# Attention's products with V in two bursts of four key tiles instead of three bursts

## Chip, cores and metric

The kernel runs on one core of one Trainium2 chip. The metric is the device time of one launch in microseconds, median of several runs; less is better.

## What is computed

The input is x, (8, 1024, 512) in float32, with a conditioning vector of 1024 for each of the 8 batch items. Two layers follow each other. The first is attention with 16 heads of 32 channels; the second is a selective state-space (Mamba) layer with 1024 inner channels and 16 states. The change touches the first alone:

```python
xn = layer_norm(x, norm_w, norm_b)
q = (xn @ q_w + q_b).reshape(Bx, Tx, H, -1)
k = (xn @ k_w + k_b).reshape(Bx, Tx, H, -1)
att = jnp.einsum('bnhl,bmhl->bnmh', q, k)
att = att + (1.0 - mask) * -1000000.0
att = jax.nn.softmax(att, axis=2)
v = ((xn @ v_w + v_b) * src_mask[:, :, None]).reshape(Bx, Tx, H, -1)
y = jnp.einsum('bnmh,bmhl->bnhl', att, v).reshape(Bx, Tx, Dx)
```

After it come a layer norm with scale and shift by the conditioning, silu, the product with out_w, the residual, and the second layer (in-projection, convolution over 4 rows, the scan over 1024 rows for 16 states, gate, out-projection).

## The kernel before, in words

Everything is float32. The 8 batch items ("instances") are worked one after the other by a loop on every engine. One instance has these stages in order: attention, norm and out-projection, norm and in-projection, convolution, dt projection, then two scan halves (dg 0 and 1) of 16 states each. Under the scan of one instance run, spread over its steps, the gate and out-projection of the instance before (dg 0) and the norm and Q, K, V products of the next one (dg 1). The queues wait for each other by semaphores written out by hand; no scheduler moves anything.

Attention is a software pipeline of 128 steps (16 heads times 8 tiles of 128 queries), which runs in step with itself on three engines. In step s:

- TensorE (line 1338 on) takes the scores of tile s: two matmuls 128x512 into one of two pairs of PSUM banks (L1316 to 1326, after the wait L1322 for the maximum of tile s-2, whose bank pair it reuses). Then it transposes the probabilities of tile s-3, eight blocks 128x128 in two quads of four (L1347), one quad for VectorE to copy out and one for ScalarE. Then come products with V (L1358 to 1361). Then, in one step of four, one transposition of the finished output (L1369).
- VectorE (L1046 on) adds the mask to the scores of tile s-1 and takes their minimum in one instruction (L1053), then, in one step of four, the normalisation of a finished output (L1063) or, in another, its copy out of PSUM (L1073) and a reciprocal (L1076), and last it copies its quad of transposed probabilities of tile s-3 (L1083).
- ScalarE (L817 on) takes the exponential of tile s-1 (L821) and copies its quad of tile s-3 (L830).

The quads go through a ring of three PSUM banks (RING, L38 on), in the order VectorE's quad of a tile, ScalarE's quad of it, and after each fourth tile one bank for the transposed output. A quad can be written when the copy of the use three places earlier is done (ring_free, L1328). So in the step after that extra use, ScalarE's quad has to wait for ScalarE's own copy of the tile before.

Four query tiles make a half (512 queries) of one head. Its product with V is y^T = V^T P^T: for each of 8 key tiles m and 4 query tiles c one matmul of V's 32 columns against a 128x128 block of P^T, into a quarter of the partitions of PSUM bank 6: 32 instructions a half. (The profile shows two records for each of them, so x24 is 12 instructions.) `AV_KEYS` (L58) says which key tiles are taken in the four steps after a half's last probabilities are copied. The four steps are named by their place in that tuple: step 0 (s mod 4 = 3) has three key tiles, step 1 three, step 2 two, step 3 none, and in step 3 the output is transposed. When key tile 7 is done, `s_av` is signalled; VectorE waits for it at L1070 before its copy L1073.

```python
                        for m in AV_KEYS[step]:
                            for c in range(HG):
                                last = mm(ps[c * HD:(c + 1) * HD, 6, 0:P], V[:, m, head * HD:(head + 1) * HD],
                                          PT[:, half % 2, m, c * P:(c + 1) * P], m, NT - 1)
                        if NT - 1 in AV_KEYS[step]:
                            last.then_inc(s_av.sem, 1)
```

L1238 is the line of the helper `mm`; the scores and the products with V both carry it and are told apart by their tiles: ps<-k_stack,q_stack is a score, ps<-area_h,area_u a product with V.

Of the kernel before, what the change touches and what calls it, by code (L numbers as in the profile page):

```python
# [54 lines left out]
def ring_bank(*use):  # L55

    return RING[RING_AT[use] % len(RING)]
AV_KEYS = ((0, 1, 2), (3, 4, 5), (6, 7), ())  # L58


N0_STEP, QKV_STEP = 13, 17
# [103 lines left out]
def build(nc, x, condT, mask, params, q_w, k_w, v_w, v_b, emb_w, emb_b, out_w, out_b,  # L165
          adaT, ada_b, inT, xpT, dtT, D_row, opT, out):
    ctx = ExitStack()
    with ctx:
# [1065 lines left out]
        def _(pe):  # L1234
# [80 lines left out]
            with pe.Fori(0, B) as b:  # L1315
# [22 lines left out]
                for s in range(ALL + Y_LAG):  # L1338
# [13 lines left out]
                    if HALF - 1 <= t < ALL + HALF - 1:  # L1352
                        half, step = (t - HALF + 1) // HALF, (t - HALF + 1) % HALF
                        head = half // 2
                        if step == 0:
                            pe.wait_ge(*s_pv.at(b, (half + 1) * HALF))
                            pe.wait_ge(*s_pa.at(b, (half + 1) * HALF))
# [6 lines that stand above are left out]
# [195 lines left out]
```

## Time and profile before

| | |
|---|---|
| median of 3 runs | 7165.17 us (7164.62 to 7170.4) |
| the profiled execution, its own time | 7160.22 us |
| its span | 7158.7 us |
| busy, share of the span | PE 88%, PEld 56%, DVE 83%, ACT 66%, POOL 44% |
| mean granted TensorE clock | 0.934 |
| products with V (x16384 records) | 603.2 us busy |
| transposes of the probabilities (x8192) | 1131.7 us busy |
| scores (x2048) | 746.7 us busy |
| masked minimum on VectorE (x1024) | 1242.5 us busy |
| exponential on ScalarE (x1024) | 1177.6 us busy |

The span is the stretch from the first to the last instruction of one execution; busy times are sums over it. PE is TensorE's matmuls (their ends are modelled), PEld its weight loads, which overlap them; DVE is VectorE, ACT ScalarE. Attention takes a stretch of some 270 us in each instance, the first from about 211 us to 487 us.

### The profile page before, as it was taken

How to read it: one execution, taken by the hardware profiler on the slowest of the kernel's cores; microseconds unless marked ns; L12 is line 12 of the kernel's file. 1: busy time of each engine (PE TensorE's matmuls, PEld its weight loads, DVE VectorE, ACT ScalarE, POOL GpSimd, SP SyncE). 2: the span in 40 equal slices, each digit the busy share in tenths (PEclk: the TensorE clock that was granted, in tenths of full speed). 3: DMA queues.
4: the chain of work that ended last, by engine and by line, in shares of the span. 5: the costliest groups of instructions: out<-in, count | busy, mean ns of one | idle time of the engine just before them, and what ended most of it. 6: DMA issues, size and time to landing. Idle time of an engine off the chain costs nothing.

```text
span 7158.7 us, 136172 instructions
## 1 busy us (share of the span) xinstructions
PE 6334.7 (88%) x43360; PEld 4004.7 (56%) x43360; DVE 5937.4 (83%) x7137; ACT 4693.5 (66%) x6673; POOL 3146.6 (44%) x1533
## 2 busy tenths in 40 slices
PE   6998799987999879989799888998799987999878
PEld 2664457644575546745467445764457544575544
DVE  0778989799896998969988799878989799896995
ACT  2665678666685667846777467766678566685664
POOL 0105771067601874018730388105771077601873
PEclk9999899998999989999799998999899998999979
DMA  3425783367923777238762487425783367823776
GB/s 142 150 91 160 178 201 118 115 160 167 238 67 135 166 173 204 72 137 189 179 169 87 137 202 186 136 96 154 178 203 115 120 158 168 233 66 136 168 174 174
DMA packets 432957, 1092.13 MB, mean 153 GB/s; under 512 B 50056, under 2 KB 50184, under 8 KB 428000
## 3 DMA queue, kind: packets, MB, share of 16 engines
q1 hardware_dynamic: 256672, 671.49, 28.5%
q0 software_dynamic: 157120, 378.04, 27.3%
q10 hardware_dynamic: 18432, 33.56, 1.3%
q8 instruction: 371, 6.08, 0.3%
q14 instruction: 362, 2.97, 0.1%
HBM read 564.39 MB, written 250.10 MB: 114 GB/s over the span
## 4 chain that ended last, share of the span: by engine, by line
PE 64%; issue 14%; DVE 8%; POOL 5%; ACT 5%; DMA 3%; SPq 1%; DVEq 1%; ACTq 0%; POOLq 0%
PE ps L1238 39%; PE ps L1483 11%; PE ps L1347 7%; POOL area_s L695 4%; PE ps L1288 3%; ACT area_h L830 2%; DVE area_h L1161 2%; DMA z_keep<-z_st 2%; DVE area_s L1053 2%; PE ps L1290 1%; ACT area_s L821 1%; DVE area_dt L1149 1%; PE ps L1432 1%; DMA area_acc<-area_w 1%; ACT k_stack L798 1%
## 5 line engine op out<-in xcount | busy, mean ns | idle before, releaser
L695 POOL TENSOR_TENSOR area_s<-area_u,area_s 128x1024 f32<-128x1024 f32 x1024 | 2536.6, 2546 | 666.3 <-DVE area_u L1152 387.0
L1161 DVE TENSOR_TENSOR_SCAN area_h<-ps,area_s 128x1024 f32<-128x1024 f32 x1024 | 2333.3, 2279 | 28.4 <-POOL area_s L695 15.0
L1483 PEld LDWEIGHTS ps<-ident,area_h 128*128 128x128 f32 x8192 | 1008.7, 151 | 961.0 <-DVE area_acc L1171 484.9
L1483 PE MATMUL ps<-ident,area_h 128*128 128x128 f32 x8192 | 1201.6, 294 | 382.1 <-DVE area_h L1161 205.7
L821 ACT ACTIVATE area_s<-area_s,negmax 128x1024 f32<-128x1024 f32 x1024 | 1177.6, 1150 | 406.6 <-DVE negmax L1053 406.1
L1053 DVE CUSTOM_DVE_ANT_0 area_s<-ps,area_dt 128x1024 f32<-128x1024 f32 x1024 | 1242.5, 1214 | 106.7 <-PE ps L1238 104.8
L888 ACT ACTIVATE ps<-area_dt,negA 128x1024 f32<-128x1024 f32 x1024 | 1145.9, 1120 | 240.3 <-DVE area_h L1161 120.9
L682 POOL TENSOR_TENSOR area_s<-area_s 128x1024 f32<-128x1024 f32 x64 | 176.1, 2752 | 2495.9 <-ACT area_s L861 2495.9
L874 ACT ACTIVATE area_w<-ps,C_nat 128x512 f32<-128x512 f32 x1024 | 703.8, 687 | 824.7 <-PE ps L1483 811.6
L1347 PE MATMUL ps<-ident,area_s 128*128 128x128 f32 x8192 | 1131.7, 277 | 35.9 <-ACT area_s L821 18.7
L1347 PEld LDWEIGHTS ps<-ident,area_s 128*128 128x128 f32 x8192 | 941.0, 142 | 267.6 <-ACT area_h L830 74.1
L1238 PE MATMUL ps<-area_xT,area_w 128*128 128x512 f32 x2176 | 1011.4, 600 | 57.9 <-ACT k_stack L798 39.4
L1171 DVE SCALAR_TENSOR_TENSOR area_acc<-ps,C_nat,area_acc 128x512 f32<-128x512 f32 x1024 | 746.4, 729 | 202.1 <-PE ps L1483 201.8
L1083 DVE COPY area_h<-ps 128x512 f32<-128x512 f32 x1024 | 705.2, 689 | 244.7 <-PE ps L1347 244.6
L1238 PE MATMUL ps<-k_stack,q_stack 128*128 128x512 f32 x2048 | 746.7, 446 | 15.3 <-DVE negmax L1053 12.1
L1238 PE MATMUL ps<-area_w,area_xT 128*128 128x512 f32 x1536 | 713.6, 600 | 0.4 <-ACT area_xT L766 0.4
L1238 PEld LDWEIGHTS ps<-area_xT,area_w 128*128 128x128 f32 x2176 | 395.3, 191 | 501.3 <-issue 356.8
L1238 PE MATMUL ps<-area_h,area_u 128*32 128x128 f32 x16384 | 603.2, 277 | 7.3 <-ACT area_h L830 7.3
L830 ACT ACTIVATE area_h<-ps 128x512 f32<-128x512 f32 x1024 | 590.4, 577 | 11.7 <-PE ps L1347 11.6
L1118 DVE SCALAR_TENSOR_TENSOR area_h<-area_h,par 128x1024 f32<-128x1024 f32 x192 | 372.6, 1940 | 167.1 <-ACT area_h L852 162.5
L1238 PEld LDWEIGHTS ps<-area_h,area_u 128*32 128x32 f32 x16384 | 401.9, 109 | 134.1 <-issue 127.0
L712 POOL DMA_DIRECT2D area_acc<-area_w x256 | 341.6, 1334 | 267.9 <-ACT area_w L874 159.7
(125 smaller groups left out, 5560.2 us busy)
## 6 DMA issues: line engine op xcount, KB each, us to landing
area_acc<-area_w POOLq DMA_DIRECT2D x256, 1024.0 KB, 8.7
area_s<-b_rows SPq DMA_DIRECT2D x256, 512.0 KB, 5.0
q_stack<-qk_keep SPq DMA_DIRECT2D x520, 128.0 KB, 2.7
k_stack<-qk_keep SPq DMA_DIRECT2D x520, 128.0 KB, 3.2
qk_keep<-q_stack SPq DMA_DIRECT2D x144, 256.0 KB, 5.0
qk_keep<-k_stack SPq DMA_DIRECT2D x144, 256.0 KB, 5.3
area_s<-z_keep SPq DMA_DIRECT2D x72, 512.0 KB, 4.5
y_keep<-area_acc POOLq DMA_DIRECT2D x8, 4096.0 KB, 14.6
```

The source lines that it names most:

```text
L695: pool.tensor_tensor(dbu[:, dl % 2, :], U[:, k // (NS * DL) * DL + dl, :], bb[:, q, :], ALU.mult).then_inc(s_dbu.sem, 1)
L821: nc.scalar.activation(S[:, t % SR, :], S[:, t % SR, :], ACT.Exp, scale=-1.0, bias=negmax[:, t % TILES:t % TILES + 1], accum_out=den[:, t ...
L830: nc.scalar.activation(PT[:, (t // HALF) % 2, HALF:NT, c * P:(c + 1) * P], ps[:, ring_bank("act", t), :].rearrange("p (m c) -> p m c", m=H ...
L874: nc.scalar.activation(part[slot][:, n // 2, :], ps[:, 5, :], ACT.Identity, scale=C_nat[:, n, columns(r, 1)]).then_inc(s_ev.sem, 1)
L888: nc.scalar.activation(banks(2 * (dl % 2)), dT[:, dl, :], ACT.Exp, scale=negA[:, a_col:a_col + 1]).then_inc(s_da.sem, 1)
L1053: v.tensor_tensor_reduce(out=S[:, t % SR, :], in0=banks(2 * (t % 2)), in1=mask_add, scale=-1.0, scalar=3.0e38, op0=ALU.add, op1=ALU.min, a ...
L1083: v.tensor_copy(PT[:, (t // HALF) % 2, 0:HALF, c * P:(c + 1) * P], ps[:, ring_bank("dve", t), :].rearrange("p (m c) -> p m c", m=HALF)).th ...
L1161: v.tensor_tensor_scan(out=hs[:, q, dl, :], data0=banks(2 * (dl % 2)), data1=dbu[:, dl % 2, :], initial=0.0, op0=ALU.mult, op1=ALU.add).th ...
L1171: v.scalar_tensor_tensor(out=part, in0=ps[:, 4, :], scalar=c_col, in1=part, op0=ALU.mult, op1=ALU.add).then_inc(s_acc.sem, 1)
L1238: return nc.tensor.matmul(out, lhsT, rhs, start=(k == 0), stop=(k == last))
L1347: last = nc.tensor.transpose(ps[:, ring_bank(who, t), m * P:(m + 1) * P], S[:, t % SR, (c * HALF + m) * P:(c * HALF + m + 1) * P], ident[: ...
L1483: last = nc.tensor.transpose(ps[:, 4 + n % 2, dl * P:(dl + 1) * P], hs[:, r % 2, dl, n * P:(n + 1) * P], ident[:, :])
```

## The change

One line, the table of key tiles by step:

```diff
@@ -55,7 +55,7 @@
-AV_KEYS = ((0, 1, 2), (3, 4, 5), (6, 7), ())
+AV_KEYS = ((0, 1, 2, 3), (), (4, 5, 6, 7), ())
```

The order of VectorE, ScalarE, GpSimd and the DMA queues is the same before and after. TensorE's order in attention, steps 1 to 3 of a half, was this before (the register instruction at L1322 is the wait ahead of the scores, the one at L1367 that ahead of the output's transposition; ps<-k_stack,q_stack are scores, ps<-ident,area_s transposes of probabilities, ps<-area_h,area_u products with V, ps<-ident,area_w the output's transposition):

```order
L1238 MATMUL ps<-k_stack,q_stack 128x512 x2
L1347 MATMUL ps<-ident,area_s 128x128 x8
L1238 MATMUL ps<-area_h,area_u 32x128 x12
L1322 REGISTER_ALU
L1238 MATMUL ps<-k_stack,q_stack 128x512 x2
L1347 MATMUL ps<-ident,area_s 128x128 x8
L1238 MATMUL ps<-area_h,area_u 32x128 x8
L1322 REGISTER_ALU
L1238 MATMUL ps<-k_stack,q_stack 128x512 x2
L1347 MATMUL ps<-ident,area_s 128x128 x8
L1367 REGISTER_ALU
L1369 MATMUL ps<-ident,area_w 128x128
```

The burst of step 0 is just ahead of the first of these rows, at x12. Of the changed kernel the same three steps read so, with a burst of x16 just ahead of the first row:

```order
L1238 MATMUL ps<-k_stack,q_stack 128x512 x2
L1347 MATMUL ps<-ident,area_s 128x128 x8
L1322 REGISTER_ALU
L1238 MATMUL ps<-k_stack,q_stack 128x512 x2
L1347 MATMUL ps<-ident,area_s 128x128 x8
L1238 MATMUL ps<-area_h,area_u 32x128 x16
L1322 REGISTER_ALU
L1238 MATMUL ps<-k_stack,q_stack 128x512 x2
L1347 MATMUL ps<-ident,area_s 128x128 x8
L1367 REGISTER_ALU
L1369 MATMUL ps<-ident,area_w 128x128
```

Step 1 has lost its burst of twelve; steps 0 and 2 hold sixteen each. The count of instructions is the same, and every matmul accumulates in the same order as before.

## Rows read from the trace of the kernel before

**Rows 1.** Busy time by stretch: span, PE, PEld, DVE, ACT, POOL busy; PEclk; DMA share, GB/s
```profile
215.00:477.00 262.00, 259.25 (x3184) 198.41 (x3183) 236.59 (x461) 212.72 (x372) 21.48 (x15) 1.00 0.30 90
...
600.00:700.00 100.00, 77.21 (x350) 46.15 (x349) 87.75 (x63) 60.59 (x71) 61.58 (x29) 0.88 0.49 130
...
1200.00:1300.00 100.00, 99.20 (x1234) 75.86 (x1225) 89.92 (x176) 80.52 (x142) 0.00 (x0) 1.00 0.23 64
```

**Rows 2.** Waits, 215 to 477 us: engine and line, releaser, us in total, times, longest
```profile
DVE area_h L1083 <- PE ps L1347: 25.3, 60, 0.5
...
PEld ps L1347 <- ACT area_h L830: 8.9, 29, 0.4
```

**Rows 3.** Timeline of PE: start, us, engine, line, op, tiles, count [idle before <-releaser]
```profile
1202.49 0.73 PE L1238 MATMUL ps<-k_stack,q_stack 128*128 128x512 f32 x2
1203.06 1.04 PE L1347 MATMUL ps<-ident,area_s 128*128 128x128 f32 x8
...
1204.02 0.64 PE L1238 MATMUL ps<-area_h,area_u 128*32 128x128 f32 x16
1204.60 0.73 PE L1238 MATMUL ps<-k_stack,q_stack 128*128 128x512 f32 x2
1205.17 1.04 PE L1347 MATMUL ps<-ident,area_s 128*128 128x128 f32 x8
...
1206.04 0.27 PE L1369 MATMUL ps<-ident,area_w 128*128 128x128 f32 x1
1206.07 0.71 PE L1238 MATMUL ps<-k_stack,q_stack 128*128 128x512 f32 x2
...
1206.64 1.35 PE L1347 MATMUL ps<-ident,area_s 128*128 128x128 f32 x8
...
1207.33 0.42 PEld L1347 LDWEIGHTS ps<-ident,area_s 128*128 128x128 f32 x4 [0.30 <-ACT area_h L830]
...
1207.92 0.86 PE L1238 MATMUL ps<-area_h,area_u 128*32 128x128 f32 x24
1208.72 0.73 PE L1238 MATMUL ps<-k_stack,q_stack 128*128 128x512 f32 x2
...
1210.25 0.86 PE L1238 MATMUL ps<-area_h,area_u 128*32 128x128 f32 x24
...
1211.04 0.73 PE L1238 MATMUL ps<-k_stack,q_stack 128*128 128x512 f32 x2
```

**Rows 4.** The same timeline, VectorE and ScalarE
```profile
1203.69 0.69 DVE L1083 COPY area_h<-ps 128x512 f32<-128x512 f32 x1 [0.49 <-PE ps L1347]
...
1204.30 1.21 DVE L1053 CUSTOM_DVE_ANT_0 area_s<-ps,area_dt 128x1024 f32<-128x1024 f32 x1
...
1205.56 1.15 ACT L821 ACTIVATE area_s<-area_s,negmax 128x1024 f32<-128x1024 f32 x1 [0.60 <-DVE negmax L1053]
...
1206.71 0.58 ACT L830 ACTIVATE area_h<-ps 128x512 f32<-128x512 f32 x1
...
1209.92 0.69 DVE L1083 COPY area_h<-ps 128x512 f32<-128x512 f32 x1 [0.34 <-PE ps L1347]
```

**Rows 5.** Timeline at the start of attention, before the first product with V
```profile
214.50 1.03 PE L1347 MATMUL ps<-ident,area_s 128*128 128x128 f32 x8
...
215.29 0.71 PE L1238 MATMUL ps<-k_stack,q_stack 128*128 128x512 f32 x2
...
217.48 1.22 DVE L1053 CUSTOM_DVE_ANT_0 area_s<-ps,area_dt 128x1024 f32<-128x1024 f32 x1
...
218.62 0.68 DVE L1083 COPY area_h<-ps 128x512 f32<-128x512 f32 x1
```

**Rows 6.** Timeline, PE: scores of steps 7 and 127, then the last burst
```profile
220.50 0.73 PE L1238 MATMUL ps<-k_stack,q_stack 128*128 128x512 f32 x2
...
477.04 0.71 PE L1238 MATMUL ps<-k_stack,q_stack 128*128 128x512 f32 x2
...
484.98 1.96 PE L1238 MATMUL ps<-area_h,area_u 128*32 128x128 f32 x64 [0.67 <-ACT area_h L830]
```

## Prediction

> **What bounds the kernel now.** I read the busy time by stretch first. In attention TensorE is busy 259.25 of 262 us at a granted clock of 1.00, the upper of its two levels (2.4 GHz), VectorE 236.59 and ScalarE 212.72 [rows 1]. TensorE seems to be the bound, but VectorE has only 10% left. Then the waits of the same stretch [rows 2]: VectorE waits for transposes 60 times (25.3 us), and TensorE's weight loads wait 29 times (8.9 us) for ScalarE's copy L830. That is two VectorE waits and one TensorE wait in a half. Attention is therefore no plain queue of TensorE work but a loop through three engines, and what counts is its longest path.
>
> The timeline gives that path. I call the starts of the scores in four steps on end X0, X1, X2 and X3, where s mod 4 is 0, 1, 2 and 3. In [rows 3] X1 is 1202.49, X2 1204.60, X3 1206.07, the next X0 1208.72 and the next X1 1211.04. The rows with x24 and x16 show which step is which: for one, the burst of 24 records at 1207.92 stands ahead of 1208.72. A step runs from one start of scores to the next: the step from X1 ends with the burst of 16, the step from X2 with the output's transposition and no burst, the steps from X3 and X0 with 24 each. (In the code's tuple the steps from X1, X2, X3 and X0 are places 2, 3, 0 and 1.) The step lengths are 2.11, 1.47, 2.65 and 2.32 us, 8.55 us for a half. The step from X3 has a bank wait inside it: its transposes take 1.35 us instead of 1.04 [rows 3], so 0.31 us.
>
> The loop that makes 8.55 us, from ScalarE's copy at 1206.71 [rows 4], which frees the bank for which TensorE waits:
> - copy 1206.71 to X0 1208.72 (rest of the transposes, burst of 24): 2.01
> - X0 to X1: 2.32
> - X1 to VectorE's copy, 1202.49 to 1203.69: 1.20
> - that copy to the next masked minimum, 1203.69 to 1204.30: 0.61
> - minimum to exponential, 1204.30 to 1205.56: 1.26
> - exponential to ScalarE's next copy, 1205.56 to 1206.71: 1.15
>
> The sum is 8.55, the measured half. In the first attention the scores of step 7 start at 220.50 and those of step 127 at 477.04 [rows 6]: 256.54 us for 30 halves, 8.55 each.
>
> **The change part by part.** No instruction is added or removed; 24 records leave the step from X0, which has none left; 8 of them go to the step from X3 (24 to 32) and 16 to the step from X1 (16 to 32).
>
> *Price of a burst of 32 records*, which attention does not show. From burst to next scores, 24 records take 0.80 (1207.92 to 1208.72) and 16 take 0.58 (1204.02 to 1204.60) [rows 3]: 0.22 for 8. So 32 take 1.02. Lower end: 0.80, the burst of 24. Upper end: two bursts of 16 with their switches, 2 x 0.58 plus the 0.17 of the next item, 1.33. I take 1.02, because the last burst of 64 records is 1.96 us long [rows 6] and the one of 24 is 0.86: 1.10 for 40, or 0.22 for 8, the same slope.
>
> *Price of a step without burst and without output's transposition*: scores to transposes 0.57 (1202.49 to 1203.06), transposes to scores 0.79 at the start of attention (214.50 to 215.29) [rows 5]; 1.36 in all. Upper end: the 1.47 of the step with the output's transposition. From transposes to a burst it is 0.96 (1203.06 to 1204.02) instead of 0.79: entering a burst costs 0.17, and of the 0.58 for 16 records 0.14 is not explained by the slope (0.58 - 2 x 0.22). So each burst has about 0.31 us that its length does not set. The Trainium skill (TensorEngine Tiling (Array Packing), Key Properties) says that changing the tiling mode, not just the tile, drains TensorE. By that rule alone the change removes one visit to the 32-column mode in each half; with the 0.31 us of the rows and the old bank wait kept, a half would fall to 8.24, close to what the sum below gives by another path. No row shows the drain itself, only the 0.31 us.
>
> *TensorE's own floor afterwards*: step from X3 2.65 - 0.31 + 0.22 = 2.56, from X1 2.11 + 0.44 = 2.55, from X2 1.47, from X0 1.36: 7.94 us without any wait. Before, it was 2.34 + 2.32 + 2.11 + 1.47 = 8.24.
>
> *The old loop afterwards*: 2.01 + 0.22, then 1.36 for X0 to X1, then 1.20 + 0.61 + 1.26 + 1.15: 7.81. It no longer decides.
>
> *The loop that takes its place* goes through VectorE's queue. The step from X0 is now so short that VectorE can't finish its turn in it: its turn is 0.61 for the copy and 1.14 for the minimum (217.48 to 218.62) [rows 5], 1.75 back to back. Path: ScalarE's copy to X0, 2.23; X0 to VectorE's copy, 1208.72 to 1209.92 [rows 4], 1.20; copy to minimum 0.61; minimum to the next copy 1.14, now without waiting for transposes; copy to minimum 0.61; minimum to exponential 1.26; exponential to ScalarE's copy 1.15. The sum is **8.20 us**. (In the kernel before the same path is 7.98, below 8.55.) It is above the floor of 7.94, so a bank wait of about 0.26 us stays at the same place.
>
> So a half goes from 8.55 to 8.20, 0.35 less. 30 halves in each of 8 instances are 240: -84 us. The first seven steps hold no product with V and the tail of five steps after the last scores has one switch less, at most 0.31 us an instance, some -2 us. What else could be touched: VectorE's wait L1070 for `s_av`. The last burst in the step from X1 now ends 0.44 later against X1 (2.55 instead of 2.11), while VectorE gets to L1073 at X1 + 1.20 + 0.61 + 1.14 = 2.95 or, late by the new loop, 3.34. The margin is 0.4 us or more, so it costs nothing; if it were gone, VectorE's copy and then TensorE's next transposes would be late. The stack loads on SP's queue are released by scores and have a whole head (eight steps, over 16 us) to land; nothing is moved past them. After attention every stage starts with TensorE's or VectorE's last attention work, so it starts earlier by the same amount and I see no transfer that would hold it.
>
> Sum: 7160.22 - 86 = 7074 us for the profiled execution. The median is 4.95 us above that execution: 7165.17 - 86 = **7079 us**, 1.2% faster. About 0.2% (14 us) is what a measurement of this kernel can tell from no change.
>
> **The rivals.**
> 1. *TensorE's floor alone.* If VectorE's lateness of 0.39 us (X0 to the second minimum 1.20 + 0.61 + 1.14 + 0.61 = 3.56, against 1.36 + 1.20 + 0.61 = 3.17) is absorbed somewhere, a half is 7.94: 0.61 x 240 = -146 us, with the tail -148, so 7017 us. For it: VectorE's busy share leaves room. Against it: every link of the new loop is a start-to-start distance that the trace shows, and the same kind of sum gave 8.55 exactly.
> 2. *A burst of 32 costs like two of 16.* At 1.33 the steps from X3 and X1 are 2.34 + 0.53 = 2.87 and 2.11 + 0.75 = 2.86, the floor is 8.56, and nothing is won: 7168 us (+0.01 x 240 = +2). The burst of 64 in [rows 6] speaks against it.
> 3. *Slower: the granted clock falls.* TensorE would work in two lumps with a thin step between. The clock is 1.00 in attention with PE busy 99% [rows 1], and in a stretch where PE is busy 77% it is 0.88. If all TensorE work of attention ran at 0.88, the floor would be 7.94 / 0.88 = 9.02, +0.47 x 240 = +113 us, 7278 us. It turns slower below 7.94 / 8.55 = 0.93. Against it: TensorE's bank wait is 0.26 in 8.20 after and 0.31 in 8.55 before, the same share.
>
> **How the numbers follow.** The VectorE loop has 0.80, the floor alone 0.12, the price of two bursts 0.04, the clock 0.04. The predicted time is that of the loop, 7079. Its own range: the burst's price enters the loop once and the slopes leave 0.99 to 1.05, and each of seven links is read to 0.01, together 0.07 a half or 17 us: 7062 to 7096. The unknown's own ends reach from 7026 (at 0.80 the loop is 7.98) to 7168; I take in half of the lower side and a little of the upper: 7040 to 7100. That leaves out some 2 in 10. Faster by over 0.2%: loop and floor, 0.92. Within 0.2%: 0.04. Slower: 0.04.
>
> **What the profile afterwards would show.** Bursts of x32 with 1.02 us to the next scores; a half of 8.20 us; step lengths from X1 on about 2.55, 1.47, 2.82 (with the bank wait) and 1.36. VectorE waits for transposes once in a half instead of twice, and in the step from X1 its copy follows the minimum at once. The wait of TensorE's weight loads for L830 stays at 29 or so times an attention, 0.3 us each. If the half is 7.9 and that wait is gone, rival 1 is right; if x32 takes 1.3, rival 2; if PEclk in attention is below 0.93, rival 3. The forecast is wrong if time appears outside attention, as an idle stretch at its end that eats the gain.

## The result and the profile after

The changed kernel takes 7082.68 us in the median of 4 runs (7079.03 to 7087.21); the kernel before, measured beside it, 7164.9 us (7163.94 to 7170.4). The ratio is 0.9884, with a 95% interval of 0.9867 to 0.9901: faster by 1.2%. The forecast was 7079. The profiled execution has a span of 7083.9 us (own time 7085.44) against 7158.7, 74.8 us less, where the sum had said 86.

Busy time by stretch, changed kernel, the part of the first attention that answers to the 262 us of [rows 1] (span; PE, PEld, DVE, ACT, POOL busy; PEclk; DMA share, GB/s):

```profile
215.00:467.00 252.00, 250.14 (x3190) 200.04 (x3188) 235.13 (x460) 213.86 (x374) 21.50 (x15) 1.00 0.32 93
```

and the waits of the same stretch (engine and line, releaser, us in total, times, longest), which answers to [rows 2]:

```profile
DVE area_h L1083 <- PE ps L1347: 16.2, 30, 0.6
PEld ps L1347 <- ACT area_h L830: 8.1, 29, 0.3
```

The clock stayed at 1.00. VectorE waits for transposes 30 times instead of 60, once in a half; TensorE still waits 29 times for ScalarE's copy, 0.28 us each (8.1 us in 29) instead of 0.31 (8.9 in 29). The work of VectorE is nearly the same (235.13 us) in 252 us instead of 262: 93% busy instead of 90%.

TensorE's timeline in one half, in the manner of [rows 3] (start, us, engine, line, op, tiles, count):

```profile
1196.69 0.71 PE L1238 MATMUL ps<-k_stack,q_stack 128*128 128x512 f32 x2
...
1199.21 0.73 PE L1238 MATMUL ps<-k_stack,q_stack 128*128 128x512 f32 x2
...
1200.69 0.71 PE L1238 MATMUL ps<-k_stack,q_stack 128*128 128x512 f32 x2
...
1201.26 1.32 PE L1347 MATMUL ps<-ident,area_s 128*128 128x128 f32 x8
...
1201.92 0.42 PEld L1347 LDWEIGHTS ps<-ident,area_s 128*128 128x128 f32 x4 [0.27 <-ACT area_h L830]
...
1202.51 1.08 PE L1238 MATMUL ps<-area_h,area_u 128*32 128x128 f32 x32
...
1203.52 0.73 PE L1238 MATMUL ps<-k_stack,q_stack 128*128 128x512 f32 x2
...
1204.87 0.71 PE L1238 MATMUL ps<-k_stack,q_stack 128*128 128x512 f32 x2
```

X1 is 1196.69, X2 1199.21, X3 1200.69, X0 1203.52, X1 1204.87. The step lengths are 2.52, 1.48, 2.83 and 1.35, together 8.18 us; the forecast was 2.55, 1.47, 2.82 and 1.36. A burst of 32 records takes 1.01 us to the next scores (1202.51 to 1203.52), where I had 1.02. VectorE and ScalarE in the same half, in the manner of [rows 4]:

```profile
1196.54 0.69 DVE L1083 COPY area_h<-ps 128x512 f32<-128x512 f32 x1 [0.54 <-PE ps L1347]
...
1197.14 1.21 DVE L1053 CUSTOM_DVE_ANT_0 area_s<-ps,area_dt 128x1024 f32<-128x1024 f32 x1
...
1198.28 0.69 DVE L1083 COPY area_h<-ps 128x512 f32<-128x512 f32 x1
...
1198.89 1.21 DVE L1053 CUSTOM_DVE_ANT_0 area_s<-ps,area_dt 128x1024 f32<-128x1024 f32 x1
...
1200.14 1.16 ACT L821 ACTIVATE area_s<-area_s,negmax 128x1024 f32<-128x1024 f32 x1
...
1201.29 0.58 ACT L830 ACTIVATE area_h<-ps 128x512 f32<-128x512 f32 x1
...
1204.72 0.69 DVE L1083 COPY area_h<-ps 128x512 f32<-128x512 f32 x1 [0.53 <-PE ps L1347]
```

In the step from X1 VectorE goes from minimum (1197.14) to copy (1198.28) in 1.14 us with no wait between; its only waits are those of 0.54 and 0.53 us in the step from X0. The forecast loop, read off these rows: ScalarE's copy 1201.29 to X0 1203.52 2.23, X0 to VectorE's copy 1204.72 1.20, copy to minimum 0.60, minimum to copy 1.14, copy to minimum 0.61, minimum to exponential 1.25, exponential to ScalarE's copy 1.15. That is 8.18. It is not one lucky half: the median over 232 neighbouring pairs of scores X1, all instances together, is 8.19 us, and 8.55 in the kernel before.

Over the whole first attention the scores of steps 7 and 127 stand at

```profile
220.43 0.73 PE L1238 MATMUL ps<-k_stack,q_stack 128*128 128x512 f32 x2
```

```profile
466.07 0.72 PE L1238 MATMUL ps<-k_stack,q_stack 128*128 128x512 f32 x2
...
477.07 0.33 PE L1369 MATMUL ps<-ident,area_w 128*128 128x128 f32 x1 [1.30 <-DVE area_w L1073]
```

so 30 halves take 245.64 us, 8.19 each, 10.90 less than in [rows 6]. (The row at 477.07 is the last transposition of an output, used below.)

**Stage by stage.** Read from the starts of each stage's first and last instructions in both traces and added over the 8 instances: from the first to the last masked minimum of attention 2175.3 us before and 2090.6 after, 84.7 less; from there to the last transposition of an output 71.3 and 69.7, 1.6 less. So attention gave 86.3 us, where the sum had 86. The stage after it, up to the last transposition of norm 2, grew from 363.1 to 381.5 us, 18.4 more, and the next, in-projection and convolution, fell from 568.6 to 561.2. The rest agrees within 2 us. In this pair of executions about 11 us of the gain was given back right behind attention. From the last output transposition to the in-projection it looks like this in the kernel before:

```profile
488.23 0.33 PE L1369 MATMUL ps<-ident,area_w 128*128 128x128 f32 x1 [1.30 <-DVE area_w L1073]
490.96 3.28 PE L1260 MATMUL ps<-ident,area_dt 128*128 128x128 f32 x16 [2.40 <-DVE area_dt L1024]
...
535.74 35.46 PE L1238 MATMUL ps<-area_xT,area_w 128*128 128x512 f32 x82 [1.64 <-ACT area_xT L766]
```

That is 47.51 us (488.23 to 535.74), and in the changed kernel (477.07 above to the row below) 49.30:

```profile
526.37 34.17 PE L1238 MATMUL ps<-area_xT,area_w 128*128 128x512 f32 x79 [1.08 <-ACT area_xT L766]
```

No instruction of this stage was changed. The granted clock did change. Here are two stretches of 10 us that hold most of the transposes of norm 1 and the second half of those of norm 2, kernel before (PEclk is the third number from the end):

```profile
491.00:501.00 10.00, 7.82 (x35) 6.72 (x36) 5.00 (x15) 6.83 (x10) 0.00 (x0) 0.69 0.56 211
531.00:541.00 10.00, 7.22 (x29) 4.12 (x30) 1.09 (x4) 4.46 (x7) 0.00 (x0) 1.00 1.02 359
```

and the same two after:

```profile
480.00:490.00 10.00, 7.64 (x34) 6.65 (x34) 4.84 (x15) 6.97 (x11) 0.00 (x0) 0.52 0.55 204
520.00:530.00 10.00, 6.98 (x25) 4.83 (x26) 1.90 (x5) 5.49 (x8) 0.00 (x0) 0.83 1.03 358
```

The mean clock is 0.69 before and 0.52 after in the stretch of norm 1, 1.00 and 0.83 in that of norm 2. The upper level is 2.4 GHz, the lower 1.2. Over the whole stage, last transposition of an output to last transposition of norm 2, the mean of the 8 instances is 0.91 before and 0.87 after. What TensorE did ahead of it is the same in both: work with idle stretches of 0.67 [rows 6], 1.30 and 2.40 us (the rows of the kernel before, above) while VectorE and ScalarE finish the last half and the norm. The instructions are the same; what had changed is when attention ends. That this moment decides is not shown. The stage also differs between instances of one execution, 44.91 to 45.81 us before and 45.59 to 48.45 after. And in two kernels below, `dve_turn0` and `dve_turn1`, whose halves are those of the changed kernel to 0.01 us (median), it took 371.5 and 373.2 us in all. So of the 18.4 us at least 8 are nothing that every kernel with these halves pays; the size belongs to this one execution.

### The profile page after: what moved, and what is told of

Read it like the earlier page. It is cut to its first block, busy times and chain, and to the rows that moved or that the text cites. A ratio compares the mean times of both kernels' runs of the same rounds, so it can differ in the third digit from the quotient of the medians.

```text
span 7083.9 us, 136172 instructions
## 1 busy us (share of the span) xinstructions
PE 6262.8 (88%) x43360; PEld 4025.1 (57%) x43360; DVE 5919.7 (84%) x7137; ACT 4697.4 (66%) x6673; POOL 3146.7 (44%) x1533
## 4 chain that ended last, share of the span: by engine, by line
PE 73%; issue 8%; DVE 6%; POOL 4%; ACT 4%; DMA 3%; SPq 0%; ACTq 0%; DVEq 0%; POOLq 0%
PE ps L1238 43%; PE ps L1347 12%; PE ps L1483 11%; POOL area_s L695 4%; PE ps L1288 3%; DVE area_h L1161 2%; DMA z_keep<-z_st 2%; PE ps L1290 1%; DMA area_acc<-area_w 1%; ACT area_h L830 1%; DVE area_dt L1149 1%; PE ps L1432 1%; ACT k_stack L798 1%; DVE area_u L1152 1%; DVE area_dt L1024 1%
## 5 line engine op out<-in xcount | busy, mean ns | idle before, releaser
L1238 PE MATMUL ps<-area_h,area_u 128*32 128x128 f32 x16384 | 551.8, 276 | 7.3 <-ACT area_h L830 7.3
L1238 PEld LDWEIGHTS ps<-area_h,area_u 128*32 128x32 f32 x16384 | 416.9, 109 | 92.6 <-issue 85.6
```

The costliest lines, as they stand in the source:

```text
L1238: return nc.tensor.matmul(out, lhsT, rhs, start=(k == 0), stop=(k == last))
```

## The experiments

Four kernels move key tiles, five put work on VectorE's queue, and two put work on TensorE in the norms. Several ran once; they are named as such, the time beside them is that of the one execution, and what is read from them is the length of a half in their trace.

**Which burst counts.** `keys305`:

```diff
-AV_KEYS = ((0, 1, 2, 3), (), (4, 5, 6, 7), ())
+AV_KEYS = ((0, 1, 2), (), (3, 4, 5, 6, 7), ())
```

> Key tiles 3, none, 5, none: two bursts as in the change, but the one in the step from X3 (on VectorE's loop) has 24 records instead of 32, the one in the step from X1 (off it) 40. Loop theory: a half falls from 8.19 to about 7.98 us (one burst of 8 records less, 0.22, on the loop), TensorE's floor stays at 7.94, the bank wait before ScalarE's quad shrinks from 0.28 to about 0.05; time about 7083 - 50 = 7033 us. Rival (only the number of visits to the 32-column mode counts): two bursts as before, so 8.19 and 7083 us.

Measured: 7032.88 us (7030.5 to 7037.36, 4 runs), ratio to the kernel before 0.9816 (0.9799 to 0.9832). TensorE's timeline of `keys305`:

```profile
1197.91 0.71 PE L1238 MATMUL ps<-k_stack,q_stack 128*128 128x512 f32 x2
1198.48 1.11 PE L1347 MATMUL ps<-ident,area_s 128*128 128x128 f32 x8
...
1203.18 1.30 PE L1238 MATMUL ps<-area_h,area_u 128*32 128x128 f32 x40
...
1205.88 0.71 PE L1238 MATMUL ps<-k_stack,q_stack 128*128 128x512 f32 x2
```

A half is 7.97 us (1197.91 to 1205.88). The transposes in the step from X3, 1.32 us long in the changed kernel, now take 1.11: the bank wait is 0.07. Two bursts, the same 64 records, the same count of switches, and 0.21 less because eight records left the loop. The rival that counts visits falls. No other version of the study is measurably faster.

`keys323`, one execution, three bursts as before the change:

```diff
-AV_KEYS = ((0, 1, 2, 3), (), (4, 5, 6, 7), ())
+AV_KEYS = ((0, 1, 2), (3, 4), (5, 6, 7), ())
```

> Key tiles 3, 2, 3, none: three bursts as in the kernel before, one key tile moved from the step from X0 to the step from X1. Loop theory: the old loop loses 0.22 and gives 8.33 us a half, above TensorE's floor of 8.24; time about 7165 - 53 = 7112 us. Rival (number of visits): three bursts, 8.55 us, 7165 us.

Measured: 7114.37 us. Two neighbouring scores X3:

```profile
1205.61 0.72 PE L1238 MATMUL ps<-k_stack,q_stack 128*128 128x512 f32 x2
...
1213.95 0.71 PE L1238 MATMUL ps<-k_stack,q_stack 128*128 128x512 f32 x2
```

That is 8.34 us for a half (forecast 8.33), with three visits. So 0.21 of the gain is to be had without removing any visit, by taking one key tile off the step from X0.

`keys503`, one execution:

```diff
-AV_KEYS = ((0, 1, 2, 3), (), (4, 5, 6, 7), ())
+AV_KEYS = ((0, 1, 2, 3, 4), (), (5, 6, 7), ())
```

> Key tiles 5, none, 3, none: two bursts, the longer one on VectorE's loop. Loop theory: 8.19 + 0.22 = 8.41 us a half, bank wait about 0.5 us; time about 7083 + 53 = 7136 us. Rival (number of visits): 8.19 us and 7083 us.

Measured: 7126.95 us.

```profile
1192.39 0.71 PE L1238 MATMUL ps<-k_stack,q_stack 128*128 128x512 f32 x2
...
1200.80 0.71 PE L1238 MATMUL ps<-k_stack,q_stack 128*128 128x512 f32 x2
```

That is 8.41 us, as forecast. The total is 9 us under the forecast: attention took 47.6 us more than in the changed kernel (53 expected), the norms 14.1 less and the convolution 5.7 more. (Stages as above.)

`keys206`, one execution, to see where the gain ends:

```diff
-AV_KEYS = ((0, 1, 2, 3), (), (4, 5, 6, 7), ())
+AV_KEYS = ((0, 1), (), (2, 3, 4, 5, 6, 7), ())
```

> Key tiles 2, none, 6, none: the burst on VectorE's loop has 16 records, the other 48. Loop theory: that loop would be 7.76 us, but TensorE's floor stays at 7.94, and the long burst now ends about when VectorE comes for its result (X1 + 2.95), so a wait at L1073 for the last key tile appears; 7.94 to 8.04 us a half, no gain over 3, none, 5, none: 7025 to 7050 us. Rival (only the burst on VectorE's loop counts): 7.76 us, about 6983 us.

Measured: 7046.6 us, inside the range, 14 above `keys305`:

```profile
1195.02 0.71 PE L1238 MATMUL ps<-k_stack,q_stack 128*128 128x512 f32 x2
...
1197.30 1.22 DVE L1053 CUSTOM_DVE_ANT_0 area_s<-ps,area_dt 128x1024 f32<-128x1024 f32 x1
...
1198.58 0.73 PE L1238 MATMUL ps<-k_stack,q_stack 128*128 128x512 f32 x2
...
1203.03 0.72 PE L1238 MATMUL ps<-k_stack,q_stack 128*128 128x512 f32 x2
```

A half is 8.01 us (1195.02 to 1203.03). The rival's 7.76 is out: TensorE's floor holds. The wait I had named is not there, though: VectorE's copy L1073 (1201.92) starts 1.13 us after the minimum ahead of it (1200.79), without a pause. The step from X0 is 1.42 us long instead of 1.36, and its end, the scores at 1198.58, lies 1.28 after the start of the masked minimum (1197.30) whose bank pair they take over; one half on the distance is 1.28 again (1205.31 to 1206.59). The same distance stands at the start of attention in the kernel before, from the minimum at 217.48 [rows 5] to this weight load of the next scores, where the row does name the wait:

```profile
218.76 0.30 PEld L1238 LDWEIGHTS ps<-k_stack,q_stack 128*128 128x128 f32 x2 [0.38 <-DVE negmax L1053]
```

Over the 232 steady halves of `keys206` the distance from that minimum to X1 is never below 1.276 us and 1.277 in the median; in `keys305` the median is 1.48, in the changed kernel 1.92. The shortest such distance in each of the 13 traces is 1.27 to 1.28. So the 0.06 is the wait L1322 for that minimum: no row of `keys206` names it, but the scores start at the shortest distance that this wait allows, every time.

**Is VectorE's queue on the path, and where?** `dve_turn1` and `dve_turn0`, the changed kernel with a small write, one execution each:

```diff
+                    if s % HALF == 1 and HALF < s < ALL:
+                        v.memset(spare[:, :], 0.0)
                     t = s - T_LAG
                     if 0 <= t < ALL:
                         dve.wait_ge(*s_pt.at(b, 2 * t + 1))
```

(`dve_turn0` has `== 0`. `spare` is a new SBUF tile of 128x4 that nothing reads; its line is left out here.)

> The changed kernel with a small write of 128x4 on VectorE in the turn of steps with s mod 4 = 1, between the masked minimum and the copy L1083: the place where VectorE works back to back. Loop theory: its length x (0.1 to 0.17 us by the reciprocal of the same size) adds to every half, 8.19 + x, so 24 to 41 us in all. Rival (TensorE's order alone decides and VectorE has room): no change, 7083 us.

> The same small write on VectorE, but in the turn of steps with s mod 4 = 0, where VectorE waits 0.54 us for TensorE's transposes before its copy. Loop theory: it lies in that wait and costs nothing, 8.19 us a half, 7083 us within a few us. Rival (VectorE's total load counts, wherever it is): the same loss as in the turn of s mod 4 = 1.

Measured: 7086.26 and 7081.69 us. These say nothing for either theory, because the write was too short. VectorE's timeline of `dve_turn1` (lines are shifted by the added ones):

```profile
1190.85 0.06 DVE L1079 MEMSET spare<- 128x4 f32 x1
```

The write starts 0.02 after the copy's start at 1190.83 and beside it. The copy is 1.15 after its minimum's start at 1189.68, against 1.14 without the write: the write took none of the queue's time. So it was done again with an addition of 128x128, `work_turn1` and `work_turn0` on the changed kernel and `before_work_turn1` on the kernel before, one execution each (`spare` is now 128x128):

```diff
+                    if s % HALF == 1 and HALF < s < ALL:
+                        v.tensor_tensor(spare[:, :], ident[:, :], ident[:, :], ALU.add)
                     t = s - T_LAG
```

> The small write of the first try took almost no time on VectorE, so the question is put again with an addition of 128x128 elements, which by the equally large L1063 takes up about 0.2 us of the queue. The changed kernel, in the turn with s mod 4 = 1, where VectorE goes from minimum to copy without waiting. Loop theory: a half 8.19 + 0.2 = 8.39 us, about +48 us, 7131 us. Rival (TensorE's order decides): 8.19 us and 7083 us.

> The same addition in the turn with s mod 4 = 0, where VectorE waits 0.54 us for the transposes. Loop theory: hidden, 8.19 us a half, 7083 us, with VectorE's wait down to about 0.34. Rival (total load of VectorE): +48 us as in the other turn.

> The same addition in the kernel before, in the turn with s mod 4 = 1. There VectorE waits 0.49 us at that place and the old loop does not go from minimum to copy in it. Loop theory: hidden, 8.55 us a half, 7165 us. Rival (VectorE's queue was on the path before the change as well): 8.75 us and about 7213 us.

Measured: 7169.42, 7132.54 and 7202.3 us, all three far above what was expected. The halves are another matter. Timeline of `work_turn1`, two neighbouring scores X3 (the addition takes 0.29 us, of which 0.21 pass until the next instruction of the queue starts, as for L1063):

```profile
1197.85 0.71 PE L1241 MATMUL ps<-k_stack,q_stack 128*128 128x512 f32 x2
...
1206.23 0.71 PE L1241 MATMUL ps<-k_stack,q_stack 128*128 128x512 f32 x2
```

That is 8.38 us (forecast 8.39). `work_turn0`:

```profile
1194.61 0.69 DVE L1086 COPY area_h<-ps 128x512 f32<-128x512 f32 x1 [0.34 <-PE ps L1350]
...
1198.75 0.72 PE L1241 MATMUL ps<-k_stack,q_stack 128*128 128x512 f32 x2
...
1206.94 0.71 PE L1241 MATMUL ps<-k_stack,q_stack 128*128 128x512 f32 x2
```

That is 8.19 us (forecast 8.19), and VectorE's wait ahead of its copy has gone from 0.54 to 0.34: the addition is hidden in it. `before_work_turn1`:

```profile
1196.66 0.71 PE L1241 MATMUL ps<-k_stack,q_stack 128*128 128x512 f32 x2
...
1205.20 0.71 PE L1241 MATMUL ps<-k_stack,q_stack 128*128 128x512 f32 x2
```

That is 8.54 us (forecast 8.55, hidden). The medians over the 232 halves say the same: 8.39 and 8.19 us against 8.19 in the changed kernel, and 8.55 against 8.55 in the kernel before. So in the steady halves the same 0.2 us costs 0.2 at one place of VectorE's queue, nothing at another, and nothing at the first place in the kernel before. VectorE's queue between X0 and ScalarE's exponential came onto the path with the change. What made the totals miss is told in the last section.

**The clock behind attention.** `fill`, the changed kernel with spare work for TensorE where it waits in the norms:

```diff
+            def keep_busy(N, b, hf):
+                if N is n2:
+                    if hf == 0:
+                        return
+                    pe.wait_ge(*s_x1.at(b, NT))
+                for _ in range(16 if N is n1 else 20):
+                    nc.tensor.transpose(ps[:, 6 + hf, 0:P], ident[:, :], ident[:, :])
             def norm_pe(N, b):
                 for hf in range(2):
+                    keep_busy(N, b, hf)
```

> The changed kernel with 16 spare transposes of the identity (results unused) into a free bank ahead of each half of norm 1's transposes and 20 ahead of the second half of norm 2's, where TensorE waits for VectorE 2.40, 2.35 and 2.85 us. Theory that the given-back 1.8 us an instance is TensorE's granted clock after attention: if the waits are what lets it fall, the stage from the last output transposition to the last transposition of norm 2 goes from about 47.7 us to 44 or less and the time falls by 8 x 3 = 24 us or more. Rival (the stage is longer because of transfers or VectorE): no gain, or a loss of up to 8 x 1 us from the spare work.

Measured: 7074.77 us (7070.85 to 7078.22), ratio 0.9872 (0.9856 to 0.9889). Timeline of `fill`, the same stage (L1261 is the spare work):

```profile
476.77 0.33 PE L1378 MATMUL ps<-ident,area_w 128*128 128x128 f32 x1 [1.30 <-DVE area_w L1073]
477.48 1.97 PE L1261 MATMUL ps<-ident 128*128 128x128 f32 x16 [0.38 <-DVE area_u L1063]
...
516.41 2.35 PE L1261 MATMUL ps<-ident 128*128 128x128 f32 x20
...
523.04 7.13 PE L1238 MATMUL ps<-area_xT,area_w 128*128 128x512 f32 x16 [1.64 <-ACT area_xT L766]
```

From 476.77 to 523.04 it is 46.27 us, where the changed kernel took 49.30 and the kernel before 47.51. The two stretches of `fill`:

```profile
480.00:490.00 10.00, 8.05 (x53) 6.14 (x52) 4.54 (x15) 7.27 (x11) 0.00 (x0) 1.00 0.53 197
520.00:530.00 10.00, 8.36 (x29) 4.31 (x28) 0.00 (x0) 2.78 (x4) 0.00 (x0) 1.00 0.84 298
```

The clock is 1.00 in both (0.995 in the mean of the stage over the 8 instances, where it was 0.87), and the stage up to the last transposition of norm 2 is 44.36 to 44.37 us in each of the 8 instances (in the changed kernel 45.59 to 48.45): 354.9 us in all against 381.5, 26.6 less. So the clock is what made that stage longer, and TensorE's waits ahead of it and in it are what let the clock fall: more work in them made the stage shorter. The whole kernel gained only 14.6 us in the profiled spans, and 8 in the medians, where the two intervals overlap: convolution took 4.2 us more, the start of the scans 6.7 more and the second scan half 5.2 more. At the start of the scans it is the clock again, 0.86 in the changed kernel and 0.83 in `fill` in the mean of the 8 instances; over the kernels of this study that stretch, from the first transposition after the convolution to the first scan, takes from 218.0 us at 0.88 (`dve_turn0`) to 227.3 at 0.82 (`fill305`). In the convolution (1.00 in both) and the second scan half (0.84 in both) the mean clock is the same, and what takes the time there is open.

`fill305`, spare work and key tiles 3, none, 5, none:

> Spare transposes and key tiles 3, none, 5, none together. If both theories hold the gains add: 7033 - 24 = 7009 us or less. If the fill does nothing, 7033 us.

Measured: 7031.97 us (7028.34 to 7038.79), ratio 0.9814 (0.9798 to 0.9831), the same as `keys305` alone. The norm stage is 354.9 us there too, against 373.8 in `keys305`, and other stages took nearly all of it back (the start of the scans 5 us more, the second scan half 9). The forecast that the gains add is wrong.

## Why the prediction was right

- *The path.* Right, and not only in the sum: each of the seven links of the VectorE loop came out within 0.01 us, the wait at ScalarE's bank stayed (0.26 forecast, 0.28 by the waits of the weight loads), VectorE lost one of its two waits. The tail was forecast at -2 us and measured -1.6. The runs that move the bursts separate this from the count of visits to the 32-column mode: 8.34, 8.18, 8.41 and 7.97 us for a half against sums of 8.33, 8.20, 8.41 and 7.98, where visits alone would have given 8.55 for the first and one and the same value for the other three.
- *The rule of the Trainium skill* (TensorEngine Tiling (Array Packing), Key Properties: a change of tiling mode drains TensorE). By that rule and the 0.31 us of the rows a half had come to 8.24, close enough to be taken for the cause. It is not what decides here. By the sums, with three visits TensorE's floor is 8.24, so of the step from 8.55 to 8.18 the removed visit can have brought only the last 0.06; no run separates that part, and no row shows the drain itself. In `keys305` it is worth more, since 7.97 is well under 8.24 and next to the floor of 7.94 with two visits; that too is argued from the sums.
- *The price of 32 records.* 1.02 forecast, 1.01 measured; 40 records take 1.23 (1203.18 to the next scores at 1204.41 in `keys305`), still on the same slope.
- *Rival 1* (TensorE's floor, 7.94) was not reached, for the reason given: VectorE is late by its back-to-back turn. *Rivals 2 and 3* did not occur; the clock in attention stayed 1.00.
- *"It starts earlier by the same amount and I see no transfer that would hold it."* No row shows one that did, but the step was incomplete. It put what happens behind attention at nothing, and the granted clock there is not the same in every execution: in the profiled pair it took 18.4 us back in the norms, and 7.4 returned in the convolution. The prediction's own sign of being wrong, time outside attention that eats the gain, did appear, as slower work at a lower clock and not as an idle stretch; it ate an eighth of the gain. The attention term was -86 and measured -86.3; the whole was -74.8 in the profiled pair and -82.2 in the medians. So the attention term is right by its mechanism, while that the total came within 4 us of 7079 is in part luck: nothing in the sum held this term small. I had put the clock only inside attention, as a rival, and not behind it.

## What to carry to other kernels

Where several engines work in step and each shows small waits, add up start-to-start distances around each loop, including those that aren't the longest yet: the next longest is what a change will be worth. In such a pipeline it matters less how much work a step holds than on which loop it lies; here four small matmuls (eight records) moved from one step to another were worth 0.21 to 0.22 us a half (medians) in the three cases where the step lay on the longest loop, without a single instruction less. An instruction added as a test must be checked in its own row before the result is read: one was too short to take any time, another lasted up to 7.7 us instead of 0.29.

## What the runs showed of the hardware

In `work_turn1`, `work_turn0` and `before_work_turn1` the additions on VectorE cost 38, 54 and 37 us in attention beyond what the steady halves explain. The time by which single additions outlast 0.29 us adds up to 34.5, 52.4 and 36.5 us, so it is nearly all of it. In `work_turn0` the time from the first masked minimum to the last is 258.0 us in the first instance and 268.7 to 270.1 in the others, against 261.0 to 262.7 for the others in the changed kernel. Most of it falls at the start of attention, where GpSimd gates the weights with four multiplications (L667 in this kernel; the profile merges the four into one row; start, us, engine). First the first instance's addition, then the second instance:

```profile
223.34 1.73 DVE L1079 TENSOR_TENSOR spare<-ident 128x128 f32<-128x128 f32 x1
...
1068.71 9.32 POOL L667 TENSOR_TENSOR area_xT<-area_xT,area_w 128x1024 f32<-128x1024 f32 x4
...
1071.93 6.26 DVE L1079 TENSOR_TENSOR spare<-ident 128x128 f32<-128x128 f32 x1
...
1078.84 1.11 PE L1350 MATMUL ps<-ident,area_s 128*128 128x128 f32 x4 [4.89 <-DVE area_h L1086]
```

An addition of two SBUF operands that otherwise takes 0.29 us lasts 6.26 us (7.7 us at the longest of the 240) and ends as GpSimd's four multiplications end, at 1078; TensorE then waits 4.89 us for VectorE's next copy. The kernel's own VectorE instructions of that stretch, which read PSUM, kept their usual 1.21 and 0.68 us. The Trainium skill (SBUF — State Buffer, SBUF: two separate sides) says of this that a VectorE operation with two SBUF inputs and a GpSimd operation that reads SBUF take a shared pair of ports exclusively, for a whole instruction, and that the loser blocks. That the two exclude each other agrees: every addition that began under such a GpSimd instruction ended some 0.15 us after the end of one. Whether the pair is free again after one instruction came out both ways. In the first instance of all three kernels the addition ended with the multiplication under which it began (the row at 223.34: that multiplication, the second of the four, ends at 224.92), and under GpSimd's additions L678 (128x512, a few tens of us later) every one of VectorE's did the same, 1.34 us at the longest in `work_turn0`. In the other seven instances of all three kernels it was held over the rest of the four multiplications until the last one ended. What makes the difference is open. (GpSimd's spans are rough.)

The second is the clock: the norm stage, with not one instruction changed, lasted from 44.36 to 48.45 us from instance to instance, and 52 transposes of the identity, 6.2 us of spare work by the timeline of `fill` (1.97, 1.91 and 2.35), laid into TensorE's waits gave 44.36 or 44.37 us every time. What the stage gained, the kernel kept only in part.
